# du in two SBUF buffers, x_proj weights through the ring of input weights, and GpSimd on group 7 of every unit, in a selective-scan kernel

## The reference

```python
xn = layernorm(x) * (1 + scale) + shift
x_in, z = split(xn @ in_proj_w.T)                 # 1024 channels each
u = silu(causal_conv4(x_in) + conv_b)
dt_r, B, C = split(u @ x_proj_w.T, [64, 80])      # 64, 16 and 16 columns
dt = softplus(dt_r @ dt_proj_w.T + dt_proj_b)
h_t = h_(t-1) * exp(dt_t * A) + (dt_t * u_t) * B_t   # 1024 channels x 16 states, over t
y = (sum over states of h * C) + u * D
x = x + gate * ((y * silu(z)) @ out_proj_w.T)
```

## Time and profile before

| | |
|---|---|
| three runs | 2239.82, 2241.41, 2244.75 us; median 2241.41 |
| the profiled execution | 2241.37 us, its span 2239.6 |
| mean granted TensorE clock | 0.966 |
| busy, share of the span | TensorE 91%, VectorE 90%, GpSimd 79%, ScalarE 74% |
| HBM read, written | 171.91 MB, 17.30 MB |

### The profile page before, as it was taken

One profiled execution on the slowest core, in us unless ns is written; L12 is line 12 of the kernel. 1 busy time (PEld: TensorE's weight loads), 2 busy tenths in 40 slices (PEclk: granted clock), 3 DMA queues, 4 the chain that ended last, 5 costly groups with the idle time before them and its releaser, 6 DMA issues. The chain is left out here.

```text
span 2239.6 us, 30720 instructions
## 1 busy us (share of the span) xinstructions
PE 2049.0 (91%) x10240; PEld 1329.0 (59%) x10240; DVE 2006.5 (90%) x2225; ACT 1649.0 (74%) x3042; POOL 1765.1 (79%) x1013
## 2 busy tenths in 40 slices
PE   9889989989998999899989989998868899999999
PEld 3345555555545555555555555555545688888878
DVE  4899999999999999999999999999999766666666
ACT  4788887878787887878887888787676455466655
POOL 0699999999999999999999999999899422232225
PEclk9899999989999999999999999999978999999999
DMA  7623422351334143433522351334001211111113
GB/s 235 256 57 92 151 105 66 94 199 48 84 98 174 51 105 81 174 112 92 164 96 61 97 195 43 85 99 170 34 19 55 99 34 36 37 53 62 41 58 132
DMA packets 104058, 220.69 MB, mean 99 GB/s; under 512 B 11933, under 2 KB 15261, under 8 KB 103902
## 3 DMA queue, kind: packets, MB, share of 16 engines
q1 hardware_dynamic: 103902, 218.74, 31.3%
HBM read 171.91 MB, written 17.30 MB: 84 GB/s over the span
## 5 line engine op out<-in xcount | busy, mean ns | idle before, releaser
L1479 POOL TENSOR_TENSOR arena<-arena 128x1024 f32<-128x1024 f32 x512 | 1198.0, 2365 | 93.7 <-ACT arena L649 87.9
L1075 DVE TENSOR_TENSOR_SCAN arena<-ps,arena 128x512 f32<-128x512 f32 x1024 | 1239.2, 1265 | 7.3 <-ACT ps L649 6.7
L649 ACT ACTIVATE ps<-arena 128x512 f32<-128x512 f32 x1087 | 715.8, 678 | 271.1 <-DVE arena L1075 138.2
L363 PEld LDWEIGHTS ps<-keep,arena 128*128 128x128 f32 x4096 | 480.4, 145 | 264.5 <-issue 140.0
L363 PE MATMUL ps<-keep,arena 128*128 128x128 f32 x4096 | 540.2, 283 | 90.0 <-POOL arena L1479 79.2
L292 PE MATMUL ps<-arena 128*128 128x512 f32 x1024 | 465.3, 597 | 12.8 <-issue 11.7
L1060 DVE TENSOR_TENSOR arena<-ps,arena 128x1024 f32<-128x1024 f32 x378 | 459.0, 1214 | 13.8 <-PE ps L363 9.8
L1448 POOL TENSOR_TENSOR arena<-arena 128x1024 f32<-128x1024 f32 x134 | 316.8, 2364 | 15.7 <-PE ps L363 15.7
L292 PEld LDWEIGHTS ps<-arena 128*128 128x128 f32 x1024 | 186.9, 191 | 232.0 <-issue 231.6
L353 PE MATMUL ps<-arena 128*128 128x512 f32 x512 | 236.9, 603 | 2.5 <-DVE arena L1096 2.5
L649 ACT ACTIVATE arena<-ps 128x512 f32<-128x512 f32 (+2 forms) x330 | 168.0, 526 | 66.8 <-PE ps L292 51.5
(11 more groups left out here) (150 smaller groups left out, 2662.6 us busy)
## 6 DMA issues: line engine op xcount, KB each, us to landing
arena<-scr_bc SPq DMA_DIRECT2D x128, 512.0 KB, 8.4
arena<-in_inT SPq DMA_DIRECT2D x184, 256.0 KB, 2.8
arena<-arena SPq DMA_DIRECT2D x224, 128.5 KB, 2.4
arena<-in_x SPq DMA_DIRECT2D x17, 512.0 KB, 3.9
scr_x<-arena SPq DMA_DIRECT2D x32, 256.0 KB, 2.0
arena_b<-scr_x SPq DMA_DIRECT2D x16, 512.0 KB, 3.7
arena_c<-scr_x SPq DMA_DIRECT2D x32, 256.0 KB, 2.9
out<-arena_c SPq DMA_DIRECT2D x32, 256.0 KB, 2.1
```

Of the source, the lines that this page charges most:

```text
L363: last = e.matmul(YP[:, 128 * q:128 * q + 128], hb[G % R][:, i, 128 * q:128 * q + 128], ident, start=(g == 0 and i == 0 and q == 0), stop= ...
L649: return e.activation(o_, i_, f, **kw)
L1075: e.tensor_tensor_scan(H, DA[s % 4], H, h0, MUL, ADD).then_inc(v_sc)
L1479: e.tensor_tensor(H, H, Ct[:, GN * g:GN * g + GN, :], MUL).then_inc(g_w)
```

## The change

It has three parts. du gets a second SBUF buffer, used by odd units, so that du(U) waits for the copy and the GpSimd products of unit U - 2 and before. The space comes from `wxp`: for the first chunk the projection's weights lie where C will be, and for the others they come as two more pieces (numbers 24 and 25, four blocks of 128 channels each) through the ring. In EACH, group 7 takes the place of one other group in every row; the number of groups in each row stays. In TensorE's order proj now stands before z_mm of the same step, and the projection's evacuation waits for the piece count.

```diff
@@ -61,9 +61,12 @@
         u, xnT, xdbl, gbc = [None, None], [None, None], [None, None], [None, None]
         u[0], xnT[0] = sb(8, T), sb(4, T)
         xt, xe = sb(2, 514), sb(516)
-        wxp, xdbl[0], gbc[1], wdt = sb(8, 128), sb(T), sb(512), sb(1024)
-        xnT[1], win = sb(4, T), [sb(4, 128) for _ in range(4)]
+        win = [sb(4, 128) for _ in range(2)]
+        xdbl[0], gbc[1], wdt = sb(T), sb(512), sb(1024)
+        xnT[1], win = sb(4, T), win + [sb(4, 128) for _ in range(2)]
+        free = sb(2, T)
         Ct = sb(16, T)
+        wx0 = Ct[:, 0:2, :].rearrange("p a b -> p (a b)").rearrange("p (k n) -> p k n", k=8)
         dt, xr, spt, xdbl[1], xs, sz = [sb(T) for _ in range(2)], [sb(512) for _ in range(2)], sb(T), sb(T), sb(2, 512), sb(3, T)
         yt = sb(4, 128)
         gbc[0] = xdbl[1]
@@ -78,6 +81,7 @@
         An, state = sb(8, 16), sb(8, 16)
         bst, mv, rstd, nmr = sb(2, 6), sb(2, 2), sb(2), sb(2)
         S1, g1, b1, sums, sq = sb(8, 2), sb(4, 2), sb(4, 2), sb(2), sb(2)
+        spt = [spt, free[:, 0, :]]
         DA, YP, DU, BG = PS[0:4], PS[4], PS[5], PS[6:8]
         bcf = Bt.rearrange("p a b -> p (a b)")
         half = [bcf[:, 4096 * h:4096 * h + 4096].rearrange("p (k n) -> p k n", k=8) for h in range(2)] + [u[1]]
@@ -198,7 +202,7 @@
         GATE = {(1, 8): (0, 0), (2, 2): (0, 1), (2, 3): (0, 2), (2, 12): (0, 3), (36, 12): (1, 0), (38, 0): (1, 1),
                 (38, 14): (1, 2), (39, 10): (1, 3)}
 
-        EACH = ((1, 3), (1, 3), (2, 4), (1, 3), (0, 2), (0, 3, 4), (0, 3, 5), (1, 5))
+        EACH = ((1, 7), (1, 7), (2, 7), (1, 7), (0, 7), (0, 3, 7), (0, 3, 7), (1, 7))
         OWN = {1: (2, 3), 2: (), 3: (3, 5), 4: (1,), 5: (0, 2), 6: (0, 3, 5), 36: (0,), 37: (0, 3), 38: (0, 3), 39: (1,)}
         pooled = lambda U, g: U > 0 and g in OWN.get(U, EACH[U % 8])
         POOLED = [G for G in range(NU * NG) if pooled(*divmod(G, NG))]
@@ -215,6 +219,8 @@
                     WSEQ.append((c + 1, XMM[j, pr][0]))
                 if (j, pr) in CMM and c + 1 < NCH:
                     WSEQ.append((c + 1, 16 + CMM[j, pr]))
+                if (j, pr) in PROJ and c + 1 < NCH:
+                    WSEQ += [(c + 1, 24 + h) for h in (0, 1) if PROJ[j, pr][0] < 4 * h + 4 <= PROJ[j, pr][1]]
                 if ends(ZMM, j, pr) and U + ZMM[j, pr][0] < NU:
                     V = U + ZMM[j, pr][0]
                     WSEQ.append((V // 8, 8 + V % 8))
@@ -222,6 +228,7 @@
         x_no = lambda c, i: w_no[c, i]
         z_no = lambda U: w_no[U // 8, 8 + U % 8]
         c_no = lambda c, i: w_no[c, 16 + i]
+        p_no = lambda c, h: w_no[c, 24 + h]
 
         kept = lambda U: U // 8 % 4 < 3
         st_of = lambda G: G + 1 - 8 * NG * (G >= 32 * NG)
@@ -336,8 +343,16 @@
                         e.wait_ge(a_su, max(q, 5) - 2)
                     if c and q in (0, 5):
                         e.wait_ge(a_su, su_of(c) - (q == 0))
-                    last = e.matmul(P, wxp[:, q, :], u[c % 2][:, q, :], start=(q == 0), stop=(q == 7))
-                if hi == 8:
+                    if c == 0:
+                        last = e.matmul(P, wx0[:, q, :], u[0][:, q, :], start=(q == 0), stop=(q == 7))
+                        continue
+                    no = p_no(c, q // 4)
+                    if q % 4 == 0:
+                        e.wait_ge(d_win[no % 4], 16 * (no // 4 + 1))
+                    last = e.matmul(P, win[no % 4][:, q % 4, :], u[c % 2][:, q, :], start=(q == 0), stop=(q == 7))
+                    if q % 4 == 3:
+                        last.then_inc(p_w)
+                if c == 0:
                     last.then_inc(p_xp)
 
             def dt_mm(U):
@@ -434,10 +449,10 @@
                         x_mm(c + 1, *XMM[j, pr])
                     if more and (j, pr) in CMM:
                         conv_mm(c + 1, CMM[j, pr])
+                    if more and (j, pr) in PROJ:
+                        proj(c + 1, *PROJ[j, pr])
                     if (j, pr) in ZMM and U + ZMM[j, pr][0] < NU:
                         z_mm(U + ZMM[j, pr][0], *ZMM[j, pr][1:])
-                    if more and (j, pr) in PROJ:
-                        proj(c + 1, *PROJ[j, pr])
                     if c > 0 and (j, pr) in OUTM:
                         for k in range(*OUTM[j, pr]):
                             n, q = divmod(k, 8)
@@ -730,7 +745,7 @@
 
             def proj_evac(c):
                 m = c % 2
-                e.wait_ge(p_xp, c + 1)
+                e.wait_ge(*((p_w, p_no(c, 1) + 1) if c else (p_xp, 1)))
                 if c == 1:
 
                     e.wait_ge(g_gw, 4)
@@ -752,7 +767,7 @@
 
                 e.wait_ge(g_du, U)
                 e.wait_ge(v_tt, tt_no(NG * U))
-                act(DU, spt, ACT.Identity).then_inc(a_du)
+                act(DU, spt[U % 2], ACT.Identity).then_inc(a_du)
 
             def z_silu(U):
                 e.wait_ge(p_w, z_no(U) + 1)
@@ -1432,12 +1447,12 @@
             def du(U):
                 c, j = divmod(U, 8)
                 e.wait_ge(a_sp, U + 1)
-                if U > 1:
-                    e.wait_ge(a_du, U - 1)
-                if ex_no(NG * U):
-                    e.wait_ge(g_ex, ex_no(NG * U))
+                if U > 2:
+                    e.wait_ge(a_du, U - 2)
+                    if ex_no(NG * (U - 1)):
+                        e.wait_ge(g_ex, ex_no(NG * (U - 1)))
                 e.wait_ge(a_su, su_of(c))
-                e.tensor_tensor(spt, dt[U % 2], u[c % 2][:, j, :], MUL).then_inc(g_du)
+                e.tensor_tensor(spt[U % 2], dt[U % 2], u[c % 2][:, j, :], MUL).then_inc(g_du)
 
             def expand(G):
                 U, g = divmod(G, NG)
@@ -1445,7 +1460,7 @@
                 if U % 8 == 0:
                     e.wait_ge(d_B[g], 16 * (U // 8 + 1))
                 e.wait_ge(p_y, G - R + 1)
-                e.tensor_tensor(hb[G % R], spt.unsqueeze(1).broadcast_to([128, GN, T]), Bt[:, GN * g:GN * g + GN, :],
+                e.tensor_tensor(hb[G % R], spt[U % 2].unsqueeze(1).broadcast_to([128, GN, T]), Bt[:, GN * g:GN * g + GN, :],
                                 MUL).then_inc(g_ex)
 
             def gate_w(b, q):
@@ -1541,7 +1556,8 @@
                 c, i = WSEQ[no]
                 if no >= 4:
                     e.wait_ge(p_w, no - 3)
-                e.dma_start(win[no % 4], A["inT"][i]).then_inc(d_win[no % 4], 16)
+                src = A["inT"][i] if i < 24 else A["xpT"][512 * (i - 24):512 * (i - 24) + 512, :].rearrange("(k p) n -> p k n", p=128)
+                e.dma_start(win[no % 4], src).then_inc(d_win[no % 4], 16)
 
             def store_bc(c):
                 e.wait_ge(a_xd, c + 1)
@@ -1603,7 +1619,7 @@
             load_x(1)
             load_ada(0, 0, 1, 2, 3)
             stream_w(4)
-            e.dma_start(wxp, A["xpT"].rearrange("(k p) n -> p k n", p=128)).then_inc(d_ws, 16)
+            e.dma_start(wx0, A["xpT"].rearrange("(k p) n -> p k n", p=128)).then_inc(d_ws, 16)
             e.dma_start(wdt[0:65, :], A["dtT"]).then_inc(d_ws, 16)
             load_half(2, A["adaT"], 1024, d_gw)
             load_x(2)
@@ -1662,6 +1678,8 @@
                     used += 1
                 if (j, pr) in CMM and more:
                     used += 1
+                if (j, pr) in PROJ and more:
+                    used += sum(1 for h in (0, 1) if PROJ[j, pr][0] < 4 * h + 4 <= PROJ[j, pr][1])
                 if ends(ZMM, j, pr) and U + ZMM[j, pr][0] < NU:
                     used += 1
                 stream_w(used + 3)
```

## The result

The changed kernel takes 2256.93 us (median of four runs, 2253.45 to 2258.91); the kernel before took 2241.47 beside it. The ratio is 1.006, with a 95% interval of 1.0045 to 1.0074: 15.5 us slower, where 5.8 us faster were forecast and the range ended at 2247. The profiled span grew from 2239.6 to 2257.1.

What follows compares the result with a forecast made beforehand. VectorE was taken to set the pace, with only 23.1 us of waits to gain. Chunk boundaries -3.0, y_back -2.2 and unnamed waits -0.6 summed to -5.8 us: 2235.6 us, with an 8-in-10 range of 2230 to 2247.

Steps and rivals of the forecast that it cites:

- What moves on VectorE: VectorE 1.1 us later from mid-unit to step 12, even at its end; waits for something fixed in the middle shrink.
- Exponential in unit 7: VectorE's 0.65 us wait in unit 7 shrinks, in six chunks; all exponential waits from 6.7 to about 1.
- y_back: VectorE's five waits for y_back at step 11, 2.9 us in all, shrink: -2.2 us.
- du in unit 7: On GpSimd, du no longer waits for group 5's product but starts by softplus, 1.05 us sooner.
- The boundary: Between chunks: GpSimd's last multiplications and TensorE's transposes 0.6 us later, yet -0.5 at four boundaries, -3.0 in all.
- The waits that no term names: VectorE's remaining small waits, mostly in units 5 and 6 of a chunk, shrink: -0.6 us.
- GpSimd's margins of 0.7 and 0.6: GpSimd's products for unit 6, groups 0 and 3, are ready 0.7 and 0.6 us before their scans; nothing charged.
- rival 3: GpSimd's margins give way; scans wait some 1.5 us once in each of seven chunks, +10 us: 2246; chance 0.13.
- The clock: At the chunk boundary, TensorE's 10.2 us stretch at granted clock 0.50 stays as long, moving with the work.
- Rival 4: Slow clock grows, 1.7 us at each of six boundaries, +10 us: 2246; chance 0.10, late stream piece included.
- The stream: Fourteen more 256 KB weight loads stay hidden: 0 taken, at worst up to 1 us in seven chunks.
- The end of the stage: V and K weights' loads go out 7 us later, still before ScalarE reads them: 0 us.

Runs made afterwards that it cites:

- e9: Kernel before plus streamed weights and two du buffers, only row 4 of EACH changed, (0, 7) for (0, 2), units 62 and 63 as before: 2250.56 us.
- e2: Changed kernel with group 7 only in rows 0 to 3 of EACH, rows 4 to 7 as before: 2253.80 us.
- e4: Changed kernel with row 4 of EACH alone back at (0, 2): 2255.47 us.
- e1: Changed kernel with EACH as before, so only the streamed weights and two du buffers stay: 2244.84 us.
- e16: Kernel before with the streamed weights alone, EACH as before and one du buffer with its old waits: 2242.71 us.
- e5: Changed kernel with group 4's transposes put ahead of the in-projections at step 13 of unit 4 in TensorE's order: 2271.44 us.
- e13: Kernel before plus streamed weights, two du buffers, only row 7 at (1, 7), units 62, 63 as before, unit 7's z_mm at step 10 instead of 9: 2247.92 us.
- e14: Changed kernel with z_mm of unit 7 at step 10 instead of 9 in TensorE's order: 2254.30 us.
- e7: Kernel before with transposes put ahead at four places of TensorE's order, in units 2, 4, 6 and 7: 2302.87 us.
- e18: Changed kernel with three quarters of every z product left out, output no longer the reference's: 2259.79 us.

## Why the prediction was wrong

**The step that failed** is "What moves on VectorE", in its sentence that VectorE is 1.1 us later from the middle of the unit to its step 12 and even at its end, and that a wait for something fixed in the middle therefore shrinks. The shift was right, and the waits named did shrink. But I took it for a gain alone. What other engines make out of the middle of a unit (exponentials, evacuations, multiplications, transposes) is 1.1 us later as well, and VectorE, one product lighter at step 12, comes back for it at its old time. Every loop that leaves VectorE before step 12 and returns after it has 1.1 us less. The waits of before show where a loop is over its limit; the loop into unit 5 had a slack of 0.04 to 0.25 us in four chunks and showed as 1.0 us of waits in two others. It now waits 6.8, and the units at place 5 are 5.7 us longer in all. Changing row 4 alone brings that wait (e9). A rival for this was missing. Not every part of the 15.5 us has such a chain shown: units 2 and 6 stay open, and between rows 3 and 4 a lag of GpSimd takes part (e2, e4).

**The sum, term by term.**
- Copy of du, 0: its wait fell from 129.8 to 22.7 us and the time didn't. Right.
- Exponential in unit 7: gone in five chunks, 0.78 each in the table. Right, but 4.4 us of waits for exponentials are left where "about 1" was named, 1.8 of it new at the scan of step 4 of unit 6. y_back: 1.8 left of 2.9 where -2.2 was named; right in sign, half in size.
- du in unit 7: started by softplus, 12.82 us after the unit's start instead of 13.84, 1.02 sooner where 1.05 was named. Right. The timelines, GpSimd and ScalarE:

```profile
693.27 1.27 POOL L1455 TENSOR_TENSOR arena<-arena 128x512 f32<-128x512 f32 x1 [1.40 <-ACT arena L664]
...
692.59 0.60 ACT L664 ACTIVATE arena<-ps 128x512 f32<-128x512 f32 x1
```

- The boundary, -3.0 in all. The eighth group's transposes started 4.55 us later than in the earlier trace rows, of which 3.1 were there at the start of unit 15: a shift of 1.4, not 0.6. Unit 0's product waited 0.81 where 0.6 was named and 0.47 stood before. Unit 7 and the unit 0 behind it, taken together, changed by -0.9, +0.1, +1.4 and -0.7 us into chunks 1, 2, 3 and 6, where -0.5 each was named (the +1.4 holds the z_mm at the low clock), and by -0.7 over all seven boundaries. Right in sign, four times too large, and not clear of what varies by itself: unit 0 alone differs by up to 1.5 us between the kernel before and e1.

```profile
502.54 1.97 PE L378 MATMUL ps<-keep,arena 128*128 128x128 f32 x8 [0.34 <-POOL arena L1494]
...
512.88 1.22 DVE L1075 TENSOR_TENSOR arena<-ps,arena 128x1024 f32<-128x1024 f32 x1 [0.81 <-PE ps L378]
```

- The waits that no term names, -0.6, mostly in units 5 and 6: this is where the loss is. In the table unit 5's product at step 2 and unit 6's at step 14 wait 7.2 us more and unit 2's 2.5. (Unit 6's line also varies by itself: 5.7 before, 7.2 in e1.)
- GpSimd's margins of 0.7 and 0.6: measured 0.40 and 0.45 in the third chunk, and they held. "The others by 1.7 or more" was wrong: group 1 of unit 1 had 0.4 to 1.7 us in chunks 1, 2, 3, 5 and 6, and 0.1 in chunk 4. Scans waited for a product once, 0.3 us, so rival 3 did not happen.
- The clock: 10.2 us at 0.50 from 498.7, moved with the work as said, and 143 against 140 us low over the stage. Rival 4 as put did not happen, though one stretch in unit 7 and one in unit 63 cost 1.7 each.
- The stream, 0: nothing that can be told (e1, e16). A piece of xpT landed in 2.9 us, one of inT in 2.8.
- The end of the stage, 0: 2.7, of which 1.1 by the last units' groups and 1.7 by the clock. The loads indeed did not matter; y_fin and the out-projection behind it, which I had not looked at, did.
- The chances: a quarter of rivals 3 and 4 together (0.23) is 0.06, where 0.04 was added up. Nothing hangs on it.

## What to carry to other kernels

Before moving work on the engine that sets the pace, list what leaves it ahead of the new gap and comes back behind it, and read the slack of each such loop from two timelines, not from the waits: in a period in which it has 0.1 us of slack it has no line among them. In a schedule where several loops are at their limit, moving one ahead can hand its wait to the next (e5, e13, e14); of 15 variants of this change none was faster than the kernel before. And compare an experiment with its forecast wait by wait: e9's time agreed while waits that nobody had named moved by 6.9 us.

## What the hardware showed

- The same six matmuls of z_mm at the same place (unit 7) took 2.81 us in 47 of 47 cases after an idle of 1.5 to 1.6 us. After 1.9 to 2.0 they did so in 22 of 40; in the other 18 the granted clock fell to 0.50 and they took 4.5. A wait longer by 0.4 us thus cost 1.7 more in nine cases of twenty. The idle just ahead is not all of it: in e7 two of seven took 4.6 and 4.9 us after an idle of 0.83. The Trainium skill (TensorE: Matmul & The Clock Gate, Part 1: The HAM clock gate) says that activity releases the clock; that the low clock came more often behind the longer idle agrees with it.
- Taking work out of TensorE can leave the time as it is: 110 us less of its busy time in the stage came with 121 us more at 1.2 GHz (e18).
